# Query and key stacks of a decoder layer: rows ordered by dimension, then product, instead of by product, then dimension

## What is computed

```python
x = x + attn(layernorm(x))            # 16 heads of 16 dims, 1024 x 1024 scores, plus a relative bias, layer norm on the output
x = x + xattn(layernorm(x), ctx)      # the same 16 heads against 77 context rows with a mask
x = x + ffn(layernorm(x))             # 8 experts of 256 x 1024 x 256, two per row, plus a shared one

# the two score products that the change touches:
attn = jnp.einsum('bhqd,bhkd->bhqk', q, k) * scale          # contraction over d = 16
scores = jnp.einsum('bhsk,bhtk->bhst', q, k)                # contraction over d = 16
```

## Time and profile before

| | |
|---|---|
| median of 3 runs | 865.16 us (863.07 to 866.2) |
| the profiled execution | 860.53 us, of it 858.4 us span |
| mean granted TensorE clock | 0.934 of full speed |
| PE / ACT / DVE / POOL busy | 87% / 47% / 43% / 16% of the span |
| chain of work that ended last | PE 72%, DMA 9%, DVE 9%, issue 3%, SP's queue 3%, ACT 3%, POOL 2% |
| DMA | 116.16 MB in 81427 packets, mean 135 GB/s |

### The profile page before, as it was taken

The page is one execution under the profiler, slowest core; times in us unless marked ns, Lnnn a source line. Parts: engine busy times, 40 slices in busy tenths (PEclk is TensorE's granted clock), DMA queues, the critical chain, the costliest instruction groups (busy, mean ns, idle before and its releaser), DMA issues.

```text
span 858.4 us, 17813 instructions
## 1 busy us (share of the span) xinstructions
PE 746.1 (87%) x6653; PEld 438.0 (51%) x6654; DVE 367.9 (43%) x1032; ACT 405.8 (47%) x509; POOL 139.8 (16%) x125
## 2 busy tenths in 40 slices
PE   1997999999999999979784897899999999999820
PEld 1463444555444444435443474666766776676610
DVE  4780221120345355476362542444444444444327
ACT  1656888887889889547151422111111111111203
POOL 5000051010000000200031233143222112212410
PEclk9997999999999999989585789999999999999965
DMA  9789989990624615193649665444445445444443
GB/s 209 176 222 156 289 136 274 243 201 3 77 32 65 86 30 76 36 232 122 74 114 252 199 235 187 136 102 126 119 100 126 118 104 121 120 111 112 80 112 98
DMA packets 81427, 116.16 MB, mean 135 GB/s; under 512 B 11164, under 2 KB 69750, under 8 KB 79028
## 3 DMA queue, kind: packets, MB, share of 16 engines
q1 hardware_dynamic: 74204, 105.79, 51.1%
q0 software_dynamic: 7152, 9.38, 6.6%
HBM read 72.81 MB, written 42.33 MB: 134 GB/s over the span
## 4 chain that ended last, share of the span: by engine, by line
PE 72%; DMA 9%; DVE 9%; issue 3%; SPq 3%; ACT 3%; POOL 2%; POOLq 0%; DVEq 0%; ACTq 0%
PE ps L1774 15%; PE ps L2085 14%; PE ps L2102 14%; PE ps L1751 13%; DMA arena<-q_parts 4%; PE ps L2093 3%; DMA q_parts<-arena 2%; SPq L499 2%; PE ps L1910 1%; DMA head_rows<-const_head_rows 1%; PE ps L1863 1%; PE ps L1827 1%; PE ps L1733 1%; PE ps L1789 1%; PE ps L1864 1%
## 5 line engine op out<-in xcount | busy, mean ns | idle before, releaser
L813 ACT ACTIVATE arena<-ps 128x1024 f32<-128x1024 f32 x256 | 241.4, 1034 | 40.6 <-PE ps L1774 39.9
L1774 PE MATMUL ps<-arena 99*32 99x512 bf16 x2048 | 168.6, 389 | 8.5 <-issue 5.2
L1751 PE MATMUL ps<-arena 128*32 128x256 f32 x2048 | 164.5, 380 | 0.7 <-issue 0.7
L2102 PE MATMUL ps<-arena,xh_tag 128*128 x560 | 128.4, 383 | 3.0 <-DVE xh_tag L1499 3.0
L2085 PE MATMUL ps<-arena 128*128 x280 | 127.9, 600 | 0.6 <-ACT arena L924 0.6
L2102 PEld LDWEIGHTS ps<-arena,xh_tag 128*128 128x128 f32 x560 | 104.9, 192 | 16.8 <-issue 3.7
L924 ACT COPY arena<-ps 128x256 f32<-128x256 f32 x35 | 13.0, 372 | 200.9 <-PE ps L2075 200.9
L731 POOL DMA_INDIRECT sums_by_row<-arena x39 | 60.3, 1547 | 229.2 <-DVE arena L1521 227.9
L1751 PEld LDWEIGHTS ps<-arena 128*32 128x32 f32 x2048 | 67.5, 111 | 53.8 <-issue 3.2
L1494 DVE TENSOR_TENSOR xh_tag<-ps,xh_tag 128x1024 f32<-128x1024 f32 x35 | 42.8, 1224 | 89.4 <-PE ps L2085 89.4
L1774 PEld LDWEIGHTS ps<-arena 99*32 99x32 bf16 x2048 | 41.3, 95 | 77.0 <-ACT arena L813 49.4
(11 more groups left out here) (239 smaller groups left out, 798.2 us busy)
## 6 DMA issues: line engine op xcount, KB each, us to landing
xh_tag<-in_L_ffn_b SPq DMA_DIRECT2D x35, 512.0 KB, 3.7
rows_by_expert<-arena SPq DMA_DIRECT2D x9, 1950.0 KB, 19.7
arena<-in_L_ffn_W SPq DMA_DIRECT2D x16, 1024.0 KB, 13.1
arena<-q_parts SPq DMA_DIRECT2D x96, 128.0 KB, 6.6
arena<-k_parts SPq DMA_DIRECT2D x48, 128.0 KB
q_parts<-arena SPq DMA_DIRECT2D x12, 384.0 KB, 2.6
arena<-rows_by_expert SPq DMA_DIRECT2D x35, 130.0 KB, 2.1
arena<-in_L_ffn_b SPq DMA_DIRECT2D x35, 128.0 KB, 3.0
```

The costliest lines, as they stand in the source:

```text
L813: nc.scalar.activation(probs_of(stage, h), ps[:, 2 * (u % 2):2 * (u % 2) + 2, :].rearrange("p a n -> p (a n)"), ACT.Exp, scale=float(D) ** ...
L1751: last = nc.tensor.matmul(ps[32 * h:32 * h + 32, 4 + half, at:at + 256], v_grp[n % 2][:, kt, h, :], probs_of(stage, h)[:, 256 * part:256 * ...
L1774: last = nc.tensor.matmul(ps[c:c + 32, 2 * (u % 2) + half, :], k_stk[buf][:, h, P * st + c:P * st + c + 32], q_stk[buf][:, h, 512 * half:5 ...
L2102: last = nc.tensor.matmul(ps[:, 6, 0:D], hid_t[:, k, :], w2_sb[:, bass.ds(e, 1), k, :].squeeze(1), start=(k == 0), stop=(k == HID // P - 1))
```

## The change

Row order in the stacks becomes "dimension, then product": the part of product `blk`, dimension `d`, goes to partition 6 * d + blk. Keys and queries get the same order, so a contraction over the 96 rows sums the same products in another order. Each read still moves 16 rows of 8 KB (5 KB in 39 KB reads) from the same DRAM addresses; it writes partitions blk, blk + 6, ..., blk + 90 where it wrote 16 * blk to 16 * blk + 15. Rows 96 to 98 stay. Number, order and size of the reads, all waits and all matmuls are as before.

```diff
--- before.py
+++ after.py
@@ -420,7 +420,7 @@
                 for stk, src, part in ((k_stk[buf], ks_dram, (0, 1, 2, 0, 1, 0)[blk]),
                                        (q_stk[buf], qs_dram, (0, 0, 0, 1, 1, 2)[blk])):
                     rows = of_heads(src[b, part, bass.ds(P * m, P), :], HG * o, HG)
-                    sp.dma_start(stk[16 * blk:16 * blk + 16, :, :], rows).then_inc(landed, 16)
+                    sp.dma_start(stk[blk:96:6, :, :], rows).then_inc(landed, 16)
 
             def load_parts(m, o, b, landed, buf):
                 for blk in range(6):
@@ -478,7 +478,7 @@
                 for blk, part in enumerate((0, 1, 2, 0, 1, 0)):
                     for m in range(KC):
                         rows = of_heads(k2_dram[part, P * m:P * (m + 1), :], 0, 8)
-                        sp.dma_start(k2_stk[DH * blk:DH * (blk + 1), 8 * m:8 * (m + 1)].rearrange("d h b t -> d h (b t)"), rows)\
+                        sp.dma_start(k2_stk[blk:6 * DH:6, 8 * m:8 * (m + 1)].rearrange("d h b t -> d h (b t)"), rows)\
                             .then_inc(k2_moved, 16)
 
             def queries_out(n):
@@ -496,7 +496,7 @@
                     queries_written(sp, n)
                 for blk, part in enumerate((0, 0, 0, 1, 1, 2)):
                     for m in range(KC):
-                        sp.dma_start(q2_stk[ch % 2][DH * blk:DH * (blk + 1), 8 * m:8 * (m + 1), :],
+                        sp.dma_start(q2_stk[ch % 2][blk:6 * DH:6, 8 * m:8 * (m + 1), :],
                                      of_heads(q2_dram[ch, part, P * m:P * (m + 1), :], 0, 8)).then_inc(q2_in[ch % 2], 16)
 
             sp.wait_ge(zeros_set, 1)
```

## The result

| | before | after |
|---|---|---|
| median of 4 runs | 864.12 us (860.54 to 866.2) | 850.51 us (848.86 to 852.56) |
| ratio, 95% interval | | 0.9848 (0.9806 to 0.989) |
| the profiled execution, its span | 860.53, 858.4 us | 849.84, 847.8 us |
| chain: PE / DMA / SP's queue | 72 / 9 / 3% | 76 / 5 / 2% |

The forecast was 849.5 us, the range 843 to 856. Against this group's median before, 13.6 us were gained where 15.7 were forecast.

What follows compares the result with a forecast made beforehand. PE's matmuls carry most of the chain, with stack reads, held up by their 16-partition destination, on the path. Terms 7.2 + 2.2 + 2.3 + 4.0 = 15.7 us take the median of 865.16 to 849.5 us; range 843 to 856.

Steps and rivals of the forecast that it cites:

- The mechanism: Stack reads: writing only 16 neighbouring partitions limits them to about 118 GB/s; spread, they nearly keep up with SP's issues.
- Part 1: Cross attention, chunk 3: PE's 14.5 us wait shrinks by whatever the last read's landing moves, 7.2 us.
- the second rival: A step of 6 partitions makes each read dearer to issue or serve, no gain above 1.10 us per read; 883 us, 4%.
- SP's issues at L499 over 0.5 us: Chunk reads' issues on SP: a named sign that the prediction is wrong; the issue took 0.42 us before.
- the prediction's lower end: Chunk 3: spread reads drain at the 64-partition rate of 210 GB/s, so the last lands 5.8 us sooner.
- Part 2: Chunk 1: PE's own last product becomes the next late thing, the division just in time; 2.2 us, bounds 1.9 and 3.0.
- part 3: Chunk 2: the reads' landing hides behind PE's output product; 2.3 us, between 1.8 and 2.95.
- Part 4: End of the projections: a queued write takes 2.9 us, not 5.44, so PE's first scores start 4.0 us sooner (1.3 to 6.3).
- Hidden, as said: Attention's other stack reads, key reads and experts' weights: they end before use or don't become the bound, so no gain counted.
- their gain goes nowhere: Attention: the other groups' faster reads save some 6 us of queue each, but PE never waits for a stack there.
- The clock rival: TensorE's clock may not fall after shorter idles at the attention's start or chunk 1, adding some 5 us; 844 us, 8%.
- the sums shift through: From chunk 3 to the experts PE, DVE and POOL hand on to each other, so earlier gains carry through unchanged.

Runs made afterwards that it cites:

- the two halves: Two kernels, each the changed kernel with only the cross attention's or only the attention's stack reads spread; 0.9869 and 0.9931 of the kernel before.
- the three steps: Spread reads writing every second, third or sixth partition (the last is the change itself); 0.9762, 0.9772 and 0.9792 of the kernel before.
- cross_only: Changed kernel with only the cross attention's reads spread, the attention's stacks as before; 855.21 us, 0.9869 of the kernel before.
- half_first: Changed kernel with chunk 3's and other chunks' query reads issued by halves of heads, PE waiting for each half separately; 845.36 us, 0.9741 of before.
- attn_only: Changed kernel with only the attention's reads spread, the cross attention's stacks as before; 859.93 us, 0.9931 of the kernel before.
- busy: Changed kernel plus unread matmuls in PE's wait for chunk 3's reads and ahead of chunk 2's last projection; 845.64 us, 0.974 of before.

## Why the prediction was right, step by step

**The mechanism** (the destination's band holds the reads up): shown by the two halves and the three steps. The landing came out at 2.4 to 3.6 us for all 48 reads, and at 2.48 for the last one of chunk 3, where 3.1 was taken. What of the destination counts is not the width of the band, by which the prediction ordered its rates: a band of 48 partitions was slower than one of 32.

**Part 1**, forecast 7.2, measured 5.6 us. The mis-sized term is the issue. The sum took the last issue's distance from the first as 450.98 - 445.99 = 4.99 us; in the kernel after it is 439.27 - 432.05 = 7.22, so 2.2 us were lost there (11 x 0.17 = 1.9 of it by the dearer issue at the median) and 0.6 us won by a landing of 2.48 in place of 3.1. The argument that failed is the one against the second rival, "count and size of the pieces don't change": they don't, and each issue became 0.17 us dearer all the same. The rival's mechanism was true at 0.64 us per read; the point from which the change would gain nothing, 1.10, was far off. The text named "SP's issues at L499 over 0.5 us" as a sign of being wrong; at 0.589 it was wrong by that sign, at the price of 2 of the 7 us of one term. The 5.6 lie next to the 5.8 of the prediction's lower end by chance: that end stood for reads that drain at 210 GB/s, and here they drained as they were issued.

**Parts 2 and 3**, forecast 4.5, measured 5.1 us up to chunk 2's first scores. The kernel after, PE at chunk 1 and at chunk 2:

```profile
366.55 1.07 PE L1875 MATMUL ps<-arena 78*32 78x512 f32 x8
367.54 0.50 PE L1863 MATMUL ps<-arena 96*78 96x512 bf16 x1
...
369.90 1.08 PE L1884 MATMUL ps<-ident,arena 128*128 128x128 f32 x4 [0.58 <-DVE arena L1319]
```

```profile
406.02 6.70 PE L1910 MATMUL ps<-arena 128*128 128x256 f32 x16 [0.68 <-ACT arena L826]
412.57 0.38 PE L1863 MATMUL ps<-arena 96*78 96x512 bf16 x1
```

Both idles (3.06 and 2.95 us) are gone wholly, which was the upper bound of both: PE shows no time for the flag any more. In chunk 1 the division that was "just in time" then comes 0.58 us late, as named.

The sum came out near, its two terms did not. The stretches from the attention's end to chunk 1's first scores and from there to chunk 2's, before and after:

```profile
355.43:378.52 23.09, 15.82 (x89) 7.46 (x88) 18.75 (x61) 10.37 (x12) 0.00 (x0) 0.87 0.75 111
378.52:424.35 45.83, 38.09 (x176) 23.23 (x177) 23.41 (x91) 20.22 (x33) 0.00 (x0) 0.80 0.61 160
```

```profile
348.73:367.54 18.81, 14.10 (x89) 6.34 (x88) 16.60 (x56) 9.67 (x11) 0.00 (x0) 1.00 0.47 124
367.54:412.57 45.03, 40.32 (x181) 25.47 (x178) 24.76 (x96) 20.91 (x34) 0.00 (x0) 0.73 0.46 169
```

Part 2 gave 4.3 us (forecast 2.2, at most 3.0), part 3 only 0.8 (forecast 2.3, at least 1.8). Beside the idle, PE was busy 1.7 us less up to chunk 1, where the clock rose from 0.87 to 1.00, and 2.2 us more behind it, where it fell from 0.80 to 0.73. That is not one trace's doing: the nine traces with spread cross reads have 18.7 to 19.5 and 43.3 to 45.0 us, the three others 23.1 to 23.4 and 45.5 to 45.8. The prediction had the clock nowhere in these two terms.

**Part 4**, forecast 4.0 us; PE's first scores come 3.4 us earlier, at 68.29, inside the named 67 to 69. The kernel after, the chain there, and then PE's first wait of all, before and after:

```profile
54.54 4.07 DMA q_parts<-arena
...
64.97 2.38 DMA arena<-shift_parts
67.35 0.94 issue
68.29 0.39 PE ps L1774 x2
68.69 2.67 issue
```

```profile
PE ps L1616 <- DMA head_rows<-const_head_rows: 16.9, 1, 16.9
```

```profile
PE ps L1616 <- DMA head_rows<-const_head_rows: 15.5, 1, 15.5
```

Of the 3.4, 1.4 us have nothing to do with the change: PE's first wait, for an input, was that much shorter, long before the first stack read. So the faster reads gave 2.0 us, half of the forecast: from the issue of that write to PE's first scores it takes 13.8 us (54.54 to 68.29) where it took 15.8 (55.87 to 71.66). This distance is 15.8 to 16.7 us in the three traces with unspread reads there and 13.0 to 13.9 in the nine with spread ones, so the gain is real; the first scores themselves lie between 67.6 and 70.8 us in the nine, six of them inside 67 to 69. The over-estimated step is the write, which still took 4.07 us where 2.9 was taken. The shift rows landed in 2.38, inside 1.9 to 4.17. The pause behind the first two matmuls stayed (2.67 us against 2.25), so the full queue is not its cause. (The upper bound of 6.3 added this pause to the 4.0 and not to the 4.5 of its own range, which would make 6.7.)

**Hidden, as said**: the key stack's reads and the experts' weights moved nothing that the traces show. **Hidden, but not free**: the attention's 3.3 us. The step that failed is "their gain goes nowhere", which looked only at waits for a stack and passed over 2.9 us of PE's idle put down to "issue".

**The clock rival**, given 8%, came true in part and at other places: up to chunk 1, as shown, and behind chunk 2's first scores. The stretch there, before and after:

```profile
424.35:434.35 10.00, 10.00 (x46) 5.04 (x47) 5.96 (x33) 6.15 (x9) 3.86 (x4) 0.70 0.12 42
```

```profile
412.60:422.60 10.00, 9.89 (x52) 4.77 (x51) 8.37 (x40) 7.32 (x10) 4.30 (x5) 1.00 0.11 41
```

The clock there was 0.70 before and 1.00 after, a matmul took 0.63 us at first and takes 0.38, and the stretch to SP's first read of chunk 3 is 2.2 us shorter. How much of that is the clock's is not shown: `cross_only` and `half_first` have 1.00 in these ten us as well and take 22.3 and 22.4 us to that read, more than the 21.64 before. Nor is it shown that the missing idle keeps the clock up, for `attn_only` has 1.1 us of idle there and 1.00 behind it. Behind chunk 3 the clock took 4.0 us away again.

**So the sum** was right partly by luck. Terms forecast at 15.7 us measured 5.6 + 5.1 + 2.0 = 12.7; 1.4 us came by chance, at the start; unforeseen gains were 3.3 and 2.2; 6.1 and 2.9 us were given back behind chunk 3 in this trace, which makes 10.6. The claim that failed is that behind chunk 3 "the sums shift through". The 2.9 us of the last stretch are no accident of one trace: it takes 328.0 to 328.9 us in all three traces of the kernel after and in `busy`, and 325.5 to 326.2 in the other eight, though its code is the same in all; why is open. The medians say 13.6 us here, 16.7 and 20.8 in two later groups; without what was given back this trace's gains would be 19.6. How much is given back on which chip is open.

## What to carry to other kernels

Where a batch of DMAs that write few partitions is waited for, try not to write neighbours. If the rows of a small stack may stand in any order, stride them: here 16 rows at a step of 2 or 6 drained as fast as they were issued (some 200 GB/s), at a step of 1 at 118 GB/s, less than half of the 285 at which they were issued. Look for it in the DMA view: engines at share 1.0 or more with few GB/s, and a landing time that grows from the first read of a batch to the last. Then check what becomes the pace, because the issue itself gets dearer (0.42 to 0.59 us here): for a batch on the path, start on the first half as soon as that has landed. And before calling a gain hidden, add up the idle time put down to "issue" beside it.

## What the runs showed of the hardware that was not expected

- SP needs 0.589 us to issue a read of 16 rows to partitions 2, 3 or 6 apart, 0.420 us for 16 neighbours (medians of 48 in each trace). It was the same for the attention's and the cross attention's reads, and for the 39 KB reads of the keys (16 rows of 2.4 KB, not of 5 KB as the section on the change has it).
- A destination over 48 partitions at a step of 3 is slower (median landing 4.3 us) than one over 32 at a step of 2 (3.0).
- DVE's chunk-3 wait of 1.6 to 2.6 us with an unnamed source came in eight of twelve traces, and of three traces of one and the same kernel in two. A single pair of traces, such as before and after here, would have put it down to the change; whether it belongs to it is open.
